# Graph network kernel: the bin builder's products, with the values put on the place one-hots in place of the column one-hots

## The chip, the cores and the metric

One core of a Trainium2 chip runs the whole kernel. The metric is the device time of one execution in microseconds (us). A core has a matrix engine (PE), a vector engine (DVE), a scalar engine (ACT), a general engine (POOL, GpSimd) and an engine that only issues transfers (SP), which run side by side and meet at semaphores.

## What is computed

Three layers of a relational graph convolution over 6,250 nodes with 128 features, 100,000 edges and 4 relations, then the input is added and a layer norm taken. For every layer:

```
for r in range(N_REL):
    mask = (edge_type == r).astype(x.dtype)
    s = segment_sum(x_src * mask[:, None], dst, num_segments=N_NODES)
    c = segment_sum(mask, dst, num_segments=N_NODES)
    mean = s / maximum(c, 1.0)[:, None]
    out = out + mean @ W[r]
```

The edges come sorted by destination. The destinations are drawn so that low node numbers have many edges each and high ones few.

## The kernel before, in words

The 100,000 edges are cut into 782 tiles of 128, and four tiles make a group. Nodes are cut into 49 blocks of 128. Each layer sums its messages in two ways.

**The gathered way** serves the edges of high destinations. POOL gathers, tile by tile, the rows of the table `ytab` (the messages x W[r] of each node and relation, in DRAM) that the edges name: line 796, one instruction a tile, 1450 in all, 550 in layer 0, 458 in layer 1 and 442 in layer 2. They land in a ring of 9 groups; POOL may overwrite a place only when PE has used it (semaphore `s_pe`). DVE builds a weighted one-hot of each tile (line 1452), PE multiplies it by the gathered rows (line 961), and DVE adds the result to the node sums (line 1474). A layer's gathers can only start when the table of that layer has been stored (lines 571 and 575).

**The dense way** serves the first 85 groups, those of low destinations. They are cut into 11 windows of destinations (5 used in layer 0, 10 in layer 1, 11 in layer 2). For a window the kernel builds the counts of edges from each source to each destination and relation (lines 1504, 1505, 1059), keeps them as f16 in DRAM (`a_dram`) for the later layers, and multiplies them with the node features (line 1043).

To build the counts of a window, its edges must first be sorted into bins by source block. This is the **bin builder**, which the change touches. A window has c slots of 128 edges for each of the 49 source blocks, so n = 49c columns: n = 147 in the first window (26 groups), 98 in the second (11 groups), 49 in the others (48 groups). Every edge has a column (`colc`, which slot), a place in the slot (`place[:, 0]`, 0 to 127), two values to be stored there (`vals`: the source within its block, and relation and destination), and its relation (`tmask`). For each group of four tiles:

- DVE (`bins`, lines 1486 to 1491) writes, in f16 with the four tiles innermost, the one-hot of the column (`pbe`, 4n elements a partition), the one-hot of the place (`pbp`, 512), the one-hot of the node within the window (`pbn`, 512), and then the column one-hot times each of the two values (`pbc`, twice 4n). The last two wait for `pbe` alone (`s_v3`). Two buffers alternate, so the first operation waits until PE has used the group before the last (`s_pu`).
- PE (`pe_bins`, lines 1013 and 1014) adds up, for each tile, the place one-hots (as weights, 128x128) times the 2n weighted columns into the bank `psB`, and beside them the relation mask (4 columns of weights) times `pbn`, which counts edges.

When a window's groups are through, DVE takes the bins out of `psB` (`take`, "N" in the order).

The order of all this is fixed when the program is built: `schedule` writes one list per layer of the steps S (a gathered group), P (a bin group), C (a piece of dense products), E, R, A and others, by costs and due times of its own, and all engines follow it. The bin groups 0 to 58 are built by DVE in layer 0, 59 to 81 in layer 1 and 82 to 84 in layer 2, one ahead of PE. The change does not touch `schedule`.

Of the kernel before, what the change touches and what calls it, by code (L numbers as in the profile page):

```python
# [11 lines left out]
F16 = mybir.dt.float16  # L12
F32R = mybir.dt.float32r
ALU = mybir.AluOpType
# [3 lines left out]
P = 128  # L18
D = 128
NR = 4  # L20
# [271 lines left out]
def rgcn_kernel(nc, x, src, dst, typ, weights, roots, biases, c_ident, c_iota, c_tri, c_col, c_need,  # L292
# [3 lines left out]
    NP, NG, NT, NB, NSL, TH = pl.NP, pl.NG, pl.NT, pl.NB, pl.NSL, pl.TH  # L296
# [12 lines left out]
    NPB = 2  # L309
# [13 lines left out]
    width = [c * NB for _, _, c in pl.win]  # L323
# [78 lines left out]
    with ctx:  # L402
        sb = lambda name, shape, dt=F32: ctx.enter_context(nc.sbuf_tensor(name, shape, dt))
# [19 lines left out]
        irep = sb("irep", [P, 4 * max([P] + width)], F16)  # L423
# [16 lines left out]
        vals = sb("vals", [P, 2, TH], F16)  # L440
        colc = sb("colc", [P, TH], F16)
        place = sb("place", [P, 2, TH], F16)
# [19 lines left out]

        WB = W * NB
        OH = NO * ((1 + NR) * P + 4) // 2
        PBW = 8 * P + 8 * max(width)
        V = sb("V", [P, max(NR * P + OH + 2 * max(width) + NPB * PBW // 2, 4 * WB + 4 * TH + P // 2 + 4 * (NP + 2) + TH // 2)])
        cap, tot, offs, adj = (V[:, i * WB:(i + 1) * WB] for i in range(4))
        blk, tmpi, tmp2 = (V[:, 4 * WB + i * TH:4 * WB + (i + 1) * TH].bitcast(I32) for i in range(3))
        relw = V[:, 4 * WB + 3 * TH:4 * WB + 4 * TH]
        ident16 = V[:, 4 * WB + 4 * TH:4 * WB + 4 * TH + P // 2].bitcast(F16)  # L470
        rowt = V[0:2, 4 * WB + 4 * TH + P // 2:4 * WB + 4 * TH + P // 2 + 4 * (NP + 2)].rearrange("r (a b c) -> r a b c", a=2, b=2)
        blk16 = V[:, 4 * WB + 4 * TH + P // 2 + 4 * (NP + 2):4 * WB + 4 * TH + P // 2 + 4 * (NP + 2) + TH // 2].bitcast(F16)
        ms = V[:, 0:NR * P]
        oh = V[:, NR * P:NR * P + OH].bitcast(F16).rearrange("p (v c) -> p v c", v=NO)
        ohs, ohk = oh[:, :, 0:P + 1], oh[:, :, P + 2:(1 + NR) * P + 3]


        by4 = lambda z: z.rearrange("p (c i) -> p c i", i=4)
        PB0 = NR * P + OH + 2 * max(width)
        pbe = lambda n: by4(V[:, NR * P + OH:NR * P + OH + 2 * n].bitcast(F16))  # L480
        pb = V[:, PB0:PB0 + NPB * PBW // 2].bitcast(F16).rearrange("p (v c) -> p v c", v=NPB)
        pbp = lambda v: by4(pb[:, v, 0:4 * P])
        pbn = lambda v: by4(pb[:, v, 4 * P:8 * P])
        pbc = lambda v, n: by4(pb[:, v, 8 * P:8 * P + 8 * n])
        st = sb("st", [P, 4, 6])
        mv = sb("mv", [P, 4, 2])
        sd = sb("sd", [P, 4])
# [40 lines left out]
        psD, psB = ps("psD", [P, 512]), ps("psB", [P, 512])  # L528
# [8 lines left out]
        q = {n: sem(n) for n in names}  # L537
# [408 lines left out]
        def pe_fast(e):  # L946
# [4 lines left out]
            for li, items in enumerate(layers):  # L951
                for pos, it in enumerate(items):
                    if it[0] == "S":
# [9 lines left out]
                        last.then_inc(q["s_pe"], 1)  # L963
                    elif it[0] == "P":
                        pe_bins(e, it[1], it[2])
                    elif it[0] == "E":
                        pe_block(e, li + 1, it[1])
# [30 lines left out]
        def pe_bins(e, w, g):  # L998


            a, b, _ = pl.win[w]
            n, v = width[w], g % NPB
            if g == a and w:
                e.wait_ge(q["s_n1"], w)
                li = [li for li in range(NL) if w in pl.built[li]][0]
                taken = [v for v in range(pl.W[li]) if pl.second[li][v]]
                if taken:
                    e.wait_ge(q["s_fd"], f_no[li, ("F", taken[-1])] + 1)
            e.wait_ge(q["s_pb"], g + 1)
            for i in range(4):  # L1010
                t = 4 * g + i
                first, end = t == 4 * a, t == 4 * b - 1
                e.matmul(psB[:, 0:2 * n], pbp(v)[:, :, i], pbc(v, n)[:, :, i], start=first, stop=end, skip_group_check=True)  # L1013
                last = e.matmul(psB[0:NR, 3 * P:4 * P], tmask[:, t, :], pbn(v)[:, :, i],
                                start=False, stop=end, skip_group_check=True)
            last.then_inc(q["s_pu"], 1)
# [422 lines left out]
        def dve_fast(e):  # L1439
# [36 lines left out]
            def bins(g):  # L1476

                w = [w for w, (a, b, _) in enumerate(pl.win) if a <= g < b][0]
                n, v = width[w], g % NPB
                if g >= NPB:  # L1480
                    e.wait_ge(q["s_pu"], g - NPB + 1)
                if g:
                    e.wait_ge(q["s_pb"], g)
                of4 = lambda z, c: z[:, 4 * g:4 * g + 4].unsqueeze(1).to_broadcast([P, c, 4])
                done[0] += 1
                e.tensor_tensor(pbe(n), by4(irep[:, 0:4 * n]), of4(colc, n), ALU.is_equal).then_inc(q["s_v3"], 1)
                e.tensor_tensor(pbp(v), by4(irep[:, 0:4 * P]), of4(place[:, 0, :], P), ALU.is_equal)
                e.tensor_tensor(pbn(v), by4(irep[:, 0:4 * P]), of4(place[:, 1, :], P), ALU.is_equal)
                e.wait_ge(q["s_v3"], done[0])
                for a in range(2):  # L1490
                    last = e.tensor_tensor(pbc(v, n)[:, a * n:(a + 1) * n, :], pbe(n), of4(vals[:, a, :], n), ALU.mult)  # L1491
                last.then_inc(q["s_pb"], 1)

            built = [0]
# [70 lines left out]
            for n in range(SHEAD):  # L1565
                build(n)
            y_stored(e, 0)
            bins(0)
            lb, pending = 0, None
            for li, items in enumerate(layers):  # L1570
                for pos, it in enumerate(items):
# [3 lines left out]
                    if it[0] == "S":  # L1575
                        n = sbase[li] + it[1]
# [5 lines left out]
                    elif it[0] == "P":  # L1582
                        if it[2] + 1 < pl.G1[-1]:
                            bins(it[2] + 1)
                        ahead(li, pos)
                    elif it[0] == "N":
                        take(it[1])
                    elif it[0] == "C" and it[1] in pl.built[li]:
                        onehots(first_of[it, "end"])
                    elif it[0] == "R":  # L1590
                        k = it[1]
                        e.wait_ge(q["s_acc"], added(li, pos))
                        b = B[:, P * k:P * k + bw[k]]
                        e.tensor_scalar(b, b, 0.0, None, ALU.max).then_inc(q["s_xt"], 1)
                    elif it[0] == "X":
                        parts = x_parts(e, it)
                        e.wait_ge(q["s_xa"], x_no[it] + 1)
                        for o, s_in in parts:
                            last = e.tensor_tensor(o(1), s_in, o(0), ALU.subtract)
                        last.then_inc(q["s_xw"], 1)  # L1600
                    elif it[0] == "F":
                        w = it[1]
                        f = f_no[li, it]
                        ahead(li, pos)
                        e.wait_ge(q["s_dn"], piece_no[li, ("C", w, NPC - 1)] + 1)
                        e.wait_ge(q["s_mb"], f + 1)
                        e.tensor_tensor(ms, banks_of(li, w)[:], ms, ALU.mult).then_inc(q["s_fd"], 1)
                    elif it[0] == "L":
                        last_stage(lb, it)
                        pending = (lb, it)  # L1610
                        lb += 1
# [192 lines left out]
```

## Time and profile before

| | |
|---|---|
| median of 3 runs | 2088.03 us (2086.58 to 2091.99) |
| profiled execution, its own time | 2091.99 us |
| its span | 2090.2 us |
| granted clock of PE, mean | 0.879 |
| busy | PE 1652.7, DVE 1359.6, POOL 1480.7, ACT 1141.2 us |
| instructions | 29086 |

The span is what the profile covers; the time of an execution holds a little more. "Busy" is the time in which an engine had an instruction of the program under way. DVE's instructions overlap at their ends, so the time that a run of them takes is read from the start of its first to the start of the next operation.

### The profile page before, as it was taken

Reading aid. Unit: us, or ns where it says so; the run is one execution under the profiler, and the core shown is the slowest. Engines: PE = TensorE matmul, PEld = TensorE weight load, DVE = VectorE, ACT = ScalarE, POOL = GpSimd, SP = SyncE. Lnnn points to the kernel's source line nnn. Section 1 sums busy time; section 2 is a strip of 40 time slices with the busy share of each in tenths; the row PEclk is TensorE's granted clock in tenths of the full one; section 3 lists DMA queues with packets and bytes.
Section 4 is the critical chain, followed back from the end, with each engine's and each line's share of the span. In section 5 each row is a group of like instructions: output and inputs, shape, how many; then the busy total and the mean of one; then the engine's idle time right before and its main releaser. Section 6 shows DMA issues by size and latency. Waiting matters only on the chain.

```text
span 2090.2 us, 29086 instructions
## 1 busy us (share of the span) xinstructions
PE 1652.7 (79%) x8296; PEld 1169.6 (56%) x8296; DVE 1359.6 (65%) x4230; ACT 1141.2 (55%) x1679; POOL 1480.7 (71%) x1459
## 2 busy tenths in 40 slices
PE   6702657788899999769999988987769999997743
PEld 3402544344456666547876655655458777775543
DVE  4797866799999988424259988876234252446752
ACT  4511000144566788367858768776367677664500
POOL 1088778877777777647777777777377777777774
PEclk9955666799999999889999999999879999999855
DMA  6411222133344455487855445444488777763431
GB/s 204 159 34 34 72 61 64 58 127 104 124 140 147 157 175 188 135 276 248 269 161 172 169 146 177 159 160 162 139 274 261 236 247 249 238 217 105 142 89 51
DMA packets 169224, 330.76 MB, mean 158 GB/s; under 512 B 34704, under 2 KB 85648, under 8 KB 169060
## 3 DMA queue, kind: packets, MB, share of 16 engines
q1 hardware_dynamic: 119000, 230.27, 31.8%
q0 software_dynamic: 46400, 94.97, 16.2%
q10 hardware_dynamic: 3660, 3.60, 0.7%
q8 instruction: 71, 1.16, 0.2%
q14 instruction: 93, 0.76, 0.1%
HBM read 210.05 MB, written 118.65 MB: 157 GB/s over the span
## 4 chain that ended last, share of the span: by engine, by line
POOL 40%; DVE 21%; PE 18%; issue 14%; DMA 3%; DVEq 1%; ACTq 1%; ACT 1%; SPq 0%; POOLq 0%
POOL ring L796 40%; DVE V L1505 5%; DVE S L1452 4%; PE psB L1043 4%; PE psD L1043 3%; DVE V L1504 3%; DMA ring<-ytab,idxc 2%; PE psY L838 2%; PE psGR L961 2%; PE psRB L961 1%; DVE rows L1300 1%; DVE node L1474 1%; DVEq L1460 1%; DMA hrows<-yst 1%; PE psT L838 1%
## 5 line engine op out<-in xcount | busy, mean ns | idle before, releaser
L796 POOL DMA_INDIRECT ring<-ytab,idxc x1402 | 1410.5, 1006 | 576.1 <-issue 419.7
L1043 PE MATMUL psD<-afull,xs 128*128 128x512 f32 (+1 forms) x1862 | 618.6, 459 | 30.3 <-ACT afull L1128 11.8
L1452 DVE TENSOR_SCALAR S<-odd_f,relc,wc 128x129 f32<-128x129 f32 x1450 | 480.6, 398 | 29.3 <-PE psGR L961 20.3
L1128 ACT ACTIVATE afull<-aring 128x1024 fp32r<-128x1024 f16 (+1 forms) x375 | 367.3, 1032 | 126.5 <-PE psD L1043 54.9
L1043 PEld LDWEIGHTS psD<-afull,xs 128*128 128x128 f32 (+1 forms) x1862 | 359.5, 198 | 96.3 <-ACT afull L1178 20.0
L1505 DVE TENSOR_SCALAR V<-odd_h,recs 128x513 f16<-128x513 f16 x686 | 325.0, 474 | 0.0
L961 PE MATMUL psRB<-S,ring 128*128 128x128 f32 (+1 forms) x1440 | 224.6, 305 | 102.6 <-DMA ring<-ytab,idxc 90.5
L1178 ACT ACTIVATE afull<-psT 128x512 fp32r<-128x512 f32 x355 | 205.2, 593 | 179.6 <-PE psT L1059 177.7
L1182 ACT ACTIVATE aring<-afull 128x1024 f16<-128x1024 f32 x275 | 286.1, 1040 | 25.5 <-ACT afull L1178 0.7
L961 PE MATMUL psGR<-S,ring 128*128 128x128 f32 x1364 | 212.4, 306 | 102.3 <-DMA ring<-ytab,idxc 93.0
L961 PEld LDWEIGHTS psRB<-S,ring 128*128 128x128 f32 (+1 forms) x1440 | 205.3, 214 | 131.6 <-issue 86.4
L961 PEld LDWEIGHTS psGR<-S,ring 128*128 128x128 f32 x1364 | 195.9, 215 | 128.2 <-issue 102.5
L1504 DVE TENSOR_SCALAR V<-odd_h,recs 128x129 f16<-128x129 f16 x686 | 189.0, 276 | 25.6 <-PE psT L1059 16.1
L1043 PE MATMUL psB<-afull,xs 128*128 128x512 f32 x686 | 177.2, 407 | 21.1 <-ACT afull L1128 12.7
L1059 PE MATMUL psT<-V 128*128 128x512 f16 x451 | 170.7, 400 | 22.3 <-DVE V L1505 17.2
L1043 PEld LDWEIGHTS psB<-afull,xs 128*128 128x128 f32 x686 | 128.3, 194 | 47.8 <-issue 12.9
L1178 ACT ACTIVATE afull<-psY 128x512 fp32r<-128x512 f32 x184 | 109.1, 593 | 64.4 <-PE psY L1059 63.6
L1474 DVE TENSOR_TENSOR node<-node,psRB 128x128 f32 x192 | 55.0, 287 | 100.4 <-DVE node L1474 58.4
L1474 DVE TENSOR_TENSOR node<-node,psGR 128x128 f32 x198 | 56.8, 287 | 89.8 <-DVE node L1474 58.0
L1158 ACT ACTIVATE xs<-yst 128x512 fp32r<-128x512 f32 (+1 forms) x39 | 23.2, 596 | 167.0 <-DMA yst<-in_x 151.2
L1013 PE MATMUL psB<-V 128*128 128x98 f16 (+2 forms) x340 | 110.8, 326 | 2.2 <-DVE V L1491 2.2
L1059 PEld LDWEIGHTS psT<-V 128*128 128x128 f16 x451 | 42.9, 99 | 108.1 <-issue 58.5
(207 smaller groups left out, 1580.8 us busy)
## 6 DMA issues: line engine op xcount, KB each, us to landing
aring<-a_dram SPq DMA_DIRECT2D x180, 512.0 KB
a_dram<-aring SPq DMA_DIRECT2D x132, 512.0 KB
ytab<-yst SPq DMA_DIRECT2D x144, 256.0 KB
ring<-ytab,idxc POOLq DMA_INDIRECT x1402
hrows<-yst SPq DMA_DIRECT2D x96, 64.0 KB
yst<-hrows SPq DMA_DIRECT2D x24, 256.0 KB, 4.6
yst<-in_x SPq DMA_DIRECT2D x23, 256.0 KB, 4.2
out<-yst SPq DMA_DIRECT2D x11, 256.0 KB, 2.7
```

The source lines that it names most:

```text
L796: e.indirect_dma_start(rows_at(n, i, m), None, Y[li % 2], bass.IndirectOffsetOnAxis(ap=idxc[0:m, t:t + 1], axis=0)).then_inc(landed(n), 16)
L961: last = e.matmul(o, rows_at(n, i, m), S[0:m, n % NS, i, 0:P], start=(i == 0), stop=(i == len(tiles[g]) - 1))
L1013: e.matmul(psB[:, 0:2 * n], pbp(v)[:, :, i], pbc(v, n)[:, :, i], start=first, stop=end, skip_group_check=True)
L1043: last = e.matmul(bank[:], xs[0:m, s, i, :], a, start=(i == 0 and s == 0), stop=(i == NB - 1 and s == 1))
L1059: e.matmul(tbank(u)[:], ohs[:, v % NO, 0:P], ohk[:, v % NO, 0:NR * P], start=(j == 0), stop=(j == c - 1)).then_inc(q["s_bd"], 1)
L1128: e.activation(afull[:, n % AF, 0:m, :], aring[:, cc % AS, o:o + m, :], ACT.Copy).then_inc(q["s_cv"], 1)
L1178: e.activation(afull[:, n % AF, j, :], tbank(u)[:], ACT.Copy).then_inc(q["s_tA"], 1)
L1182: e.activation(aring[:, cc % AS, half:half + m, :], afull[:, n % AF, 0:m, :], ACT.Copy).then_inc(q["s_cv"], 1)
L1452: last = e.tensor_scalar(run3(S[:, n % NS, i, 0:P + 1]), odd128f, relc[:, t:t + 1], wc[:, t:t + 1], ALU.is_equal, ALU.mult)
L1474: e.tensor_tensor(w, w, part[bank][:, j * P:(j + 1) * P], ALU.add).then_inc(q["s_acc"], 1)
L1504: e.tensor_scalar(run3(ohs[:, v % NO, :]), odd128, recs[:, 0, at:at + 1], None, ALU.is_equal)
L1505: e.tensor_scalar(run3(ohk[:, v % NO, :]), odd512, recs[:, 1, at:at + 1], None, ALU.is_equal).then_inc(q["s_oh"], 1)
```

## The change

The two values are multiplied onto the one-hot of the place, not onto the one-hot of the column. The column one-hot (`pbc`, now 4n elements) is the streamed operand of both values, and each value has place one-hots of its own as weights (`pbp(v, 0)` and `pbp(v, 1)`). In the bin builder DVE now makes five operations of 512, 512, 4n, 512 and 512 elements, where it made 4n, 512, 512, 4n and 4n. PE now makes, for each tile, two products of n columns with different weights where it made one of 2n. The numbers that reach `psB` are the same. The buffer V is cut anew for it: `pbe` has 512 elements in place of 4n, a set of `pb` has 12P + 4n in place of 8P + 8n.

```diff
-        PBW = 8 * P + 8 * max(width)
+        PBW = 12 * P + 4 * max(width)
...
-        pbe = lambda n: by4(V[:, NR * P + OH:NR * P + OH + 2 * n].bitcast(F16))
+        pbe = by4(V[:, NR * P + OH:NR * P + OH + 2 * P].bitcast(F16))
...
-        pbp = lambda v: by4(pb[:, v, 0:4 * P])
-        pbn = lambda v: by4(pb[:, v, 4 * P:8 * P])
-        pbc = lambda v, n: by4(pb[:, v, 8 * P:8 * P + 8 * n])
+        pbp = lambda v, a: by4(pb[:, v, 4 * P * a:4 * P * (a + 1)])
+        pbn = lambda v: by4(pb[:, v, 8 * P:12 * P])
+        pbc = lambda v, n: by4(pb[:, v, 12 * P:12 * P + 4 * n])
...
-                e.matmul(psB[:, 0:2 * n], pbp(v)[:, :, i], pbc(v, n)[:, :, i], start=first, stop=end, skip_group_check=True)
+                for a in range(2):
+                    e.matmul(psB[:, a * n:(a + 1) * n], pbp(v, a)[:, :, i], pbc(v, n)[:, :, i],
+                             start=first and a == 0, stop=end, skip_group_check=True)
...
-                e.tensor_tensor(pbe(n), by4(irep[:, 0:4 * n]), of4(colc, n), ALU.is_equal).then_inc(q["s_v3"], 1)
-                e.tensor_tensor(pbp(v), by4(irep[:, 0:4 * P]), of4(place[:, 0, :], P), ALU.is_equal)
+                e.tensor_tensor(pbe, by4(irep[:, 0:4 * P]), of4(place[:, 0, :], P), ALU.is_equal).then_inc(q["s_v3"], 1)
                 e.tensor_tensor(pbn(v), by4(irep[:, 0:4 * P]), of4(place[:, 1, :], P), ALU.is_equal)
+                e.tensor_tensor(pbc(v, n), by4(irep[:, 0:4 * n]), of4(colc, n), ALU.is_equal)
                 e.wait_ge(q["s_v3"], done[0])
                 for a in range(2):
-                    last = e.tensor_tensor(pbc(v, n)[:, a * n:(a + 1) * n, :], pbe(n), of4(vals[:, a, :], n), ALU.mult)
+                    last = e.tensor_tensor(pbp(v, a), pbe, of4(vals[:, a, :], P), ALU.mult)
                 last.then_inc(q["s_pb"], 1)
```

## Rows read from the trace of the kernel before

**Rows 1.** The page, busy time by engine and the chain that ended last.

```profile
PE 1652.7 (79%) x8296; PEld 1169.6 (56%) x8296; DVE 1359.6 (65%) x4230; ACT 1141.2 (55%) x1679; POOL 1480.7 (71%) x1459
...
POOL 40%; DVE 21%; PE 18%; issue 14%; DMA 3%; DVEq 1%; ACTq 1%; ACT 1%; SPq 0%; POOLq 0%
```

**Rows 2.** Waits of POOL: engine line, waited for, us in total, times, longest.

```profile
POOL ring L796 <- issue: 419.7, 1377, 0.3
...
POOL ring L796 <- DMA hrows<-yst: 51.9, 2, 28.7
...
POOL ring L796 <- PE psGR L961: 5.5, 12, 2.0
...
POOL ring L796 <- PE psRB L961: 4.2, 10, 1.4
```

**Rows 3.** Timeline of POOL, no bins near: start, us, operation, idle before.

```profile
1401.56 0.94 POOL L796 DMA_INDIRECT ring<-ytab,idxc  x1 [0.30 <-issue]
```

**Rows 4.** The chain by line, for 389:640, 640:806 and 806:884 us.

```profile
by line: DVE V L1505 33.4%; DVE S L1452 18.8%; DVE V L1504 17.0%; issue 4.0%; DVE node L1474 3.8%; DVEq L1460 3.8%; DVE V L1491 3.2%; DVE V L1487 2.4%; DVE V L1488 2.4%; DMA ring<-ytab,idxc 1.8%; DVE V L1486 1.6%; PE psGR L961 1.2%; DVE cin
...
by line: DVE V L1505 18.1%; DVE S L1452 17.0%; PE psD L1043 11.0%; DVE V L1504 9.1%; DVE node L1474 4.5%; issue 4.4%; DVEq L1460 4.2%; PE psGR L961 4.0%; PE psT L1059 3.8%; PE psRB L961 3.4%; PE psB L1014 2.5%; PE psY L1059 2.3%; PE psT L83
...
by line: POOL ring L796 74.3%; issue 24.0%; DMA ring<-ytab,idxc 3.2%; PE psGR L961 0.7%
```

**Rows 5.** Line 796 by window: window, length, busy (count), PE clock, DMA, GB/s.

```profile
220.00:389.00 169.00, 135.17 (x112) 0.68 0.21 60
...
389.00:511.00 122.00, 94.88 (x90) 0.90 0.33 108
...
511.00:770.00 259.00, 196.79 (x195) 0.97 0.43 144
...
1048.00:1350.00 302.00, 230.74 (x234) 0.98 0.49 163
...
1350.00:1489.00 139.00, 105.17 (x112) 0.90 0.46 152
```

**Rows 6.** Timeline in layer 1, a bin group with n = 49.

```profile
1168.06 0.26 DVE L1486 TENSOR_TENSOR V<-irep,colc 128x196 f16<-128x196 f16 x1
...
1168.20 1.95 POOL L796 DMA_INDIRECT ring<-ytab,idxc  x1 [0.30 <-issue]
...
1169.24 0.28 DVE L1504 TENSOR_SCALAR V<-odd_h,recs 128x129 f16<-128x129 f16 x1
```

**Rows 7.** Timeline in layer 0, bin groups with n = 147.

```profile
342.29 0.47 DVE L1486 TENSOR_TENSOR V<-irep,colc 128x588 f16<-128x588 f16 x1 [4.23 <-PE psB L1014]
...
342.93 0.97 POOL L796 DMA_INDIRECT ring<-ytab,idxc  x1 [0.30 <-issue]
...
344.09 1.35 DVE L1452 TENSOR_SCALAR S<-odd_f,relc,wc 128x129 f32<-128x129 f32 x4
...
345.46 3.19 POOL L796 DMA_INDIRECT ring<-ytab,idxc  x1 [0.30 <-issue]
```

**Rows 8.** Timeline of DVE in layer 0, a bin group with n = 98.

```profile
442.34 0.35 DVE L1486 TENSOR_TENSOR V<-irep,colc 128x392 f16<-128x392 f16 x1
...
443.83 0.40 DVE L1452 TENSOR_SCALAR S<-odd_f,relc,wc 128x129 f32<-128x129 f32 x1
```

**Rows 9.** Groups by form on DVE: count, busy us, mean ns, idle before.

```profile
L1488 DVE TENSOR_TENSOR V<-irep,place 128x512 f16<-128x512 f16 x85 | 35.6, 419 | 0.0
...
L1491 DVE TENSOR_TENSOR V<-V,vals 128x196 f16<-128x196 f16 x96 | 20.4, 253 | 0.0
...
L1486 DVE TENSOR_TENSOR V<-irep,colc 128x588 f16<-128x588 f16 x26 | 12.0, 460 | 32.1 <-PE psB L1014 32.0
```

**Rows 10.** PE: the weight load by form, and the timeline at n = 49.

```profile
L1013 PEld LDWEIGHTS psB<-V 128*128 128x128 f16 x340 | 39.6, 117 | 44.1 <-issue 8.7 <-DVE V L1491 2.8
...
698.19 0.26 PE L1013 MATMUL psB<-V 128*128 128x98 f16 x1
...
698.38 0.28 PE L1014 MATMUL psB<-V,tmask 128*4 128x128 f16 x1
```

More of the change, by code:

```diff
@@ L464, in rgcn_kernel @@
         OH = NO * ((1 + NR) * P + 4) // 2
-        PBW = 8 * P + 8 * max(width)
-        V = sb("V", [P, max(NR * P + OH + 2 * max(width) + NPB * PBW // 2, 4 * WB + 4 * TH + P // 2 + 4 * (NP + 2) + TH // 2)])
+        PBW = 12 * P + 4 * max(width)
+        V = sb("V", [P, max(NR * P + OH + 2 * P + NPB * PBW // 2, 4 * WB + 4 * TH + P // 2 + 4 * (NP + 2) + TH // 2)])
         cap, tot, offs, adj = (V[:, i * WB:(i + 1) * WB] for i in range(4))
@@ L478, in rgcn_kernel @@
         by4 = lambda z: z.rearrange("p (c i) -> p c i", i=4)
-        PB0 = NR * P + OH + 2 * max(width)
-        pbe = lambda n: by4(V[:, NR * P + OH:NR * P + OH + 2 * n].bitcast(F16))
-        pb = V[:, PB0:PB0 + NPB * PBW // 2].bitcast(F16).rearrange("p (v c) -> p v c", v=NPB)
-        pbp = lambda v: by4(pb[:, v, 0:4 * P])
-        pbn = lambda v: by4(pb[:, v, 4 * P:8 * P])
-        pbc = lambda v, n: by4(pb[:, v, 8 * P:8 * P + 8 * n])
+        pbe = by4(V[:, NR * P + OH:NR * P + OH + 2 * P].bitcast(F16))
+        pb = V[:, NR * P + OH + 2 * P:NR * P + OH + 2 * P + NPB * PBW // 2].bitcast(F16).rearrange("p (v c) -> p v c", v=NPB)
+        pbp = lambda v, a: by4(pb[:, v, 4 * P * a:4 * P * (a + 1)])
+        pbn = lambda v: by4(pb[:, v, 8 * P:12 * P])
+        pbc = lambda v, n: by4(pb[:, v, 12 * P:12 * P + 4 * n])
         st = sb("st", [P, 4, 6])
```

## The prediction, made before the change was run

> **What bounds the kernel now.** I read the page first: no engine is busy for more than 79% of the span, and the chain that ended last is 40% GpSimd (POOL), 21% DVE, 18% PE [rows 1]. Shares do not say which of them holds the end, so I asked what POOL waits for. Over the whole run its gathers wait 52 us at the two changes of layer and only 5.5 + 4.2 us for PE to give a ring place back; all the rest before a gather is its own 0.30 us of issue, 1377 times [rows 2]. Undisturbed, a gather takes 0.94 us and 0.30 of issue ahead of it, so one starts every 1.25 us [rows 3]. So inside a layer POOL hardly ever stands still, and whatever lengthens a gather moves the end of the layer. The chain taken by stretches agrees in part: at the end of layer 0 it is POOL and issue; from 389 to 640 us it is DVE (one-hots L1504 and L1505, weighted one-hots L1452), and from 640 to 806 us DVE and PE by turns [rows 4]. I read this as DVE and PE falling behind the gathers until the ring of 9 groups is full, where the few waits of [rows 2] come from, and then catching up.
>
> **What lengthens a gather.** The windows of line 796 give its time by stage [rows 5]. Without bin building (1350 to 1489 us) 112 gathers are busy 105.2 us, 0.94 each. With it they take more; the surplus over 0.944 each, divided by the groups built there:
> - 220 to 389 us, 26 groups with n = 147: 135.2 - 105.7 = 29.4 us, 1.13 a group.
> - 389 to 511 us, 11 groups with n = 98: 94.9 - 85.0 = 9.9 us, 0.90 a group.
> - 511 to 770 us, 22 groups with n = 49: 196.8 - 184.1 = 12.7 us, 0.58 a group.
> - 1048 to 1350 us, 23 groups with n = 49: 230.7 - 220.9 = 9.8 us, 0.43 a group.
>
> The timelines show how: a gather that starts 0.14 us into the five two-input f16 operations of a bin group takes 1.95 us, not 0.94 [rows 6], and one that starts under such a run in the widest window takes 3.19, while another, started 0.64 us into its run, takes 0.97 [rows 7]. So these operations stop a gather, depending on where its start falls in the run. Groups that start in the same place of the gather's beat lose more the longer the run is: runs last (start of the first to start of the next other operation) 1.18 us at n = 49 [rows 6], 1.49 at n = 98 [rows 8], 1.80 at n = 147 [rows 7], and lose 0.50 (the mean over 45 groups, 22.5 / 45), 0.90 and 1.13. That is a slope of 1.3 us of gather per us of run, then 0.74, 1.03 over all.
>
> The Trainium skill (SBUF — State Buffer, the practical consequences) says that a DVE instruction with two SBUF inputs contends with a GpSimd instruction that reads SBUF, and that the loser is blocked until the DVE operation ends. The trace agrees as far as [rows 6] go. The same section adds that tensor_tensor was seen not to stall DMA, by inference because writing descriptors needs the other interface; by that sentence the gathers here would lose nothing before or after and the sum would be 2093 us in place of 2105, and the trace does not bear it out [rows 6].
>
> **The change on DVE.** Per group of four tiles the operations stay five. Elements before: 4n (L1486), 512 (L1487), 512 (L1488), 2 x 4n (L1491), so 1024 + 12n. After: 512, 512, 4n, 2 x 512, so 2048 + 4n. The difference is 1024 - 8n: +632 at n = 49, +240 at n = 98, -152 at n = 147. By form the 512-element operation takes 419 ns and the 196-element one 252 or 253 [rows 9]: 166 / 316 = 0.53 ns an element. The runs show the same, 0.31 us for 588 elements between n = 49 and 98, and again to 147 [rows 6 to 8]. So a run grows by 0.335 us (n = 49, 48 groups: 22 in layer 0, 23 in layer 1, 3 in layer 2), by 0.127 (n = 98, 11 groups) and shrinks by 0.081 (n = 147, 26 groups). DVE busy: 16.1 + 1.4 - 2.1 = +15.4 us.
>
> **The change on POOL.** This is the term that counts. At a slope of 1 the gathers lose what the runs gain: layer 0 gets 22 x 0.335 + 1.4 - 2.1 = 6.7 us, layer 1 7.7, layer 2 1.0, together 15.4. The bounds come from the two measured slopes. A run of n = 49 becomes 1.51 us, a hair over the n = 98 run of today that loses 0.90, so read off there the loss grows by 0.41 a group: 48 x 0.41 + 11 x 0.17 - 26 x 0.06 = 20 us. With the flat slope of 0.74: 48 x 0.25 + 1.0 - 2.2 = 11 us. I take slope 1, between them, because the number of groups behind 0.90 is only 11. Below nothing the term can go only if the places of the starts are redrawn; see the rivals.
>
> Where DVE sets the pace (389 to 640 us), its run growth, 11 x 0.127 and some ten groups x 0.335, 4.7 us, is of the same size as what POOL loses there, and the two run side by side: it is counted once.
>
> **The change on PE.** Each tile's product of 2n columns (L1013) becomes two of n with different weights. The columns that stream are the same; 340 weight loads of 128x128 are added, 117 ns each by the load's row [rows 10]: 39.8 us of PE, or 0.47 a group. If the load is hidden behind the matmul before, it costs nothing. The whole step of today's L1013 at n = 49, its load and its 98 columns, takes 0.19 us from its start to that of the next matmul (698.19 to 698.38) [rows 10], so a load that is added cannot cost more: 0.76 a group is the far end. PE is covered wherever the chain is POOL, by the ring: POOL waits for PE 9.7 us in the whole run. Without that cover it would be the 39.8 us. The one place where it is short is before 640 us in layer 0: there 11 + 10 groups x 0.47 = 9.9 us are added on PE, 5.2 more than on DVE. The chain of that stretch is DVE's and not PE's [rows 4], so I let 1.5 us through, with 0 and 5.2 as ends (at the far price of 0.76: 21 x 0.76 - 4.7 = 11.3). After it 12 x 0.47 = 5.6 us are added on PE against 4.0 on POOL, up to 1.6 more at the tail of the layer, which I leave to the range.
>
> **Costed at nothing.** The order of the operations in a group (the flag that the multiplies wait for is still that of the first), the smaller buffer V (456 bytes a partition less), the smaller PSUM regions: the same bank, the same number of waits, nothing new queued behind one. DVE's L1486 waits 32.0 us for PE to free a bin buffer in the 26 widest groups [rows 9]; PE's added loads lengthen that wait, and the gathers, which set that stage's pace, hide it (uncovered it would be 26 x 0.47 = 12 us).
>
> **Sum.** Against the profiled execution's own 2091.99 us: + 15.4 + 1.5 = 2108.9, +17 us. That execution is 4.0 us above the median of the three runs, so on the median's basis 2088.0 + 17 = 2105 us, 0.8% slower. What this kernel's measurement can tell from no change is about 0.3%, 6.3 us.
>
> **Rivals.**
> - **The steep slope**: every n = 49 group loses what n = 98 loses today. For it: the measured step from 1.18 to 1.49 us. Against: 11 groups. 20 + 1.5: 2110 us, and with the PE end 2114.
> - **PE sets the pace in layer 0**: the added loads are not hidden and both 5.2 and 1.6 us land. For it: PE is 79% busy over the span, more than DVE's 65% [rows 1]. Against: before 640 us the chain names DVE [rows 4]. 2088 + 15.4 + 6.8 = 2110 us, and 2088 + 15.4 + 11.3 = 2115 at the far price of a load.
> - **No contention from these operations**: the long gathers come from something else that falls together with the bin groups. Then POOL loses nothing more, and only the stretch that DVE paces grows, by 4.7 us: 2093 us, within 0.3%. For it: some runs leave a gather at 0.97 us [rows 7]. Against: the surplus grows with n and is nil where no bins are built [rows 5]. The Trainium skill's sentence on tensor_tensor and DMA, above, would be this case.
> - **The flat slope or less**: 11 us on POOL, nothing on PE, 2099 us; with a lucky redraw of starts (a group's loss scatters from 0.03 to 2.25 us [rows 7], about 0.7 for 85 groups, so some 6 us over all) it reaches 2093.
> - **Faster: a redraw of where the 26 widest groups meet the gathers.** They lose 29.4 us, and a run met late, like the 0.97 us gather of [rows 7], costs 0.03. The change shortens these runs and shifts everything around them. If nearly all fell that way, 2088 + 17 - 29 = 2076 us. It decides from 23 us gained, four fifths of the loss; nothing in the change aims the starts, and four times the 6 us scatter is needed.
>
> **How the numbers follow.** Forecast (2098 to 2112) 0.50, steep slope 0.15, PE 0.15, flat or less 0.12 (half of it within 0.3%), no contention 0.04, faster 0.04. Slower 0.50 + 0.15 + 0.15 + 0.06 = 0.86; same 0.10; faster 0.04. The range goes from 2093 (flat slope less the scatter, no PE, or no contention) to 2088 + 20 + 5.2 + 6, 2119 us, with a microsecond at the lower end: 2092 to 2119. The forecast's own is 2098 to 2112.
>
> **What the profile after would show.** Right: runs of the five operations of 1.51 us at n = 49; DVE busy up by 15; gathers' busy time up by 11 to 20, of it about 1 us lost a group in windows like [rows 5] against 0.50; the widest window a little better; undisturbed gathers still 1.25 us apart; POOL's wait for PE under 15 us. 340 more loads on PE and its busy time up. Wrong: gathers' busy time unchanged (no contention), POOL waiting tens of us for PE or a tail longer than 23 to 29 us at the layers' ends (PE is the bound), or the 220 to 389 us stage shorter by 20.

## The result, and the profile after

The changed kernel takes 2107.64 us at the median of four runs (2102.64 to 2108.51) and 2105.48 us at the median of all its twelve (2101.37 to 2108.51), beside 2089.23 us for the kernel before on the same occasions. The ratio, taken over the twelve, is 1.0078, 95% interval 1.0062 to 1.0093, which is 16.3 us (13.0 to 19.4) slower. The profiled execution took 2101.77 us, the second lowest of the twelve, and against the profiled execution of before (2091.99 us) it shows 9.8 us and not 16. So this one profile holds less of the change's cost than most executions do; how executions of one kernel differ is part of the story below.

The page of the changed kernel, busy time by engine and the chain by engine; they answer to [rows 1]:

```profile
PE 1663.6 (79%) x8636; PEld 1191.4 (57%) x8636; DVE 1375.2 (65%) x4230; ACT 1141.7 (54%) x1679; POOL 1486.7 (71%) x1459
...
POOL 47%; PE 17%; issue 15%; DVE 14%; DMA 3%; DVEq 1%; ACT 1%; ACTq 1%; SPq 0%; POOLq 0%
```

DVE has 15.6 us more (the sum said 15.4), PE 340 more matmuls and loads but only 10.9 us more, POOL 6.0 us more, less than the 11 to 20 that the prediction gave as a sign of being right. POOL's waits, against [rows 2]:

```profile
POOL ring L794 <- DMA hrows<-yst: 53.6, 2, 28.5
...
POOL ring L794 <- PE psGR L959: 6.1, 12, 2.7
POOL ring L794 <- PE psRB L959: 2.7, 7, 0.8
```

8.8 us of waiting for PE after, 9.7 before: PE is no more in the way than it was. (Lines shift: the gather is line 794 now, the gathered products 959, the bin products 1012. DVE's L1486 makes the one-hot of the place now, L1487 that of the node, L1488 that of the column.) The gathers by stage, the stages cut where the bin groups of the changed kernel start and end, against [rows 5]:

```profile
221.00:384.00 163.00, 128.87 (x113) 0.66 0.22 63
384.00:504.00 120.00, 92.89 (x90) 0.90 0.34 109
504.00:767.00 263.00, 201.87 (x192) 0.96 0.42 141
1050.00:1357.00 307.00, 236.31 (x233) 0.97 0.48 159
1357.00:1497.00 140.00, 105.86 (x113) 0.91 0.46 154
```

The last row is a stage without bins, 0.94 us a gather as before. In the others take 0.944 us for each gather off the busy time and divide by the groups, as before:

| stage | surplus before | after | a group, before | after |
|---|---|---|---|---|
| n = 147, 26 groups | 29.4 us | 22.2 | 1.13 | 0.85 |
| n = 98, 11 groups | 9.9 | 7.9 | 0.90 | 0.72 |
| n = 49, layer 0, 22 groups | 12.7 | 20.6 | 0.58 | 0.94 |
| n = 49, layer 1, 23 groups | 9.8 | 16.4 | 0.43 | 0.71 |

An n = 49 group costs the gathers 0.82 us (37.0 / 45) where it cost 0.50: +0.32, where the forecast said 0.335. The widest groups cost 7 us less in all, where it said 2. The ends of a window cut gathers in two, which moves a surplus by up to about 2 us; and the four surpluses together grow by only 5.3 us here, since the 7.2 and 2.0 us less of the wide groups stand against 7.9 and 6.6 more.

A bin group with n = 49 in layer 1, timelines of DVE and of POOL, against [rows 6]:

```profile
1113.14 0.42 DVE L1486 TENSOR_TENSOR V<-irep,place 128x512 f16<-128x512 f16 x1
1113.48 0.42 DVE L1487 TENSOR_TENSOR V<-irep,place 128x512 f16<-128x512 f16 x1
1113.81 0.26 DVE L1488 TENSOR_TENSOR V<-irep,colc 128x196 f16<-128x196 f16 x1
1113.98 0.76 DVE L1491 TENSOR_TENSOR V<-V,vals 128x512 f16<-128x512 f16 x2
1114.65 0.28 DVE L1504 TENSOR_SCALAR V<-odd_h,recs 128x129 f16<-128x129 f16 x1
```

```profile
1113.32 2.24 POOL L794 DMA_INDIRECT ring<-ytab,idxc  x1 [0.30 <-issue]
1115.87 0.94 POOL L794 DMA_INDIRECT ring<-ytab,idxc  x1 [0.30 <-issue]
```

The run lasts 1.51 us (1113.14 to 1114.65), 1.18 before. The gather that starts 0.18 us into it ends at 1115.56, 0.91 us after the run is over. The gather of [rows 6] ended at 1170.15, and its run at 1169.24: 0.91 us again. A gather that is caught like this does not share the time with the run: its last 0.91 us come after the run. So its length follows the run's end: 0.33 us more of run and a start 0.04 us later make 0.29 us more of gather.

On PE, the tile of the changed kernel at n = 49, against [rows 10]:

```profile
1112.38 0.15 PEld L1012 LDWEIGHTS psB<-V 128*128 128x128 f16 x2
1112.38 0.27 PE L1012 MATMUL psB<-V 128*128 128x49 f16 x2
...
1112.58 0.08 PEld L1014 LDWEIGHTS psB<-V,tmask 128*4 128x4 f16 x1
```

Both products together take 0.20 us from their start to that of the next matmul, where the one product took 0.19. Over all tiles of the two traces the medians are 0.194 us against 0.191 at n = 49, 0.279 against 0.277 at n = 98 and 0.367 against 0.365 at n = 147. The second load costs the stream next to nothing.

### The profile page after: what moved, and what is told of

It reads as the page before. It is cut to its first block, busy times and chain, and to the rows that moved or that the text cites. A ratio compares the mean times of both kernels' runs of the same rounds, so it can differ in the third digit from the quotient of the medians.

```text
span 2099.9 us, 29766 instructions
## 1 busy us (share of the span) xinstructions
PE 1663.6 (79%) x8636; PEld 1191.4 (57%) x8636; DVE 1375.2 (65%) x4230; ACT 1141.7 (54%) x1679; POOL 1486.7 (71%) x1459
## 4 chain that ended last, share of the span: by engine, by line
POOL 47%; PE 17%; issue 15%; DVE 14%; DMA 3%; DVEq 1%; ACT 1%; ACTq 1%; SPq 0%; POOLq 0%
POOL ring L794 44%; DVE V L1505 5%; PE psD L1043 4%; PE psB L1043 3%; DVE S L1452 3%; POOL rows L794 3%; PE psY L836 3%; DVE V L1504 3%; DMA ring<-ytab,idxc 2%; PE psGR L959 2%; PE psRB L959 1%; DVEq L1460 1%; PE psT L836 1%; DVE node L1474 1%; DMA hrows<-yst 1%
## 5 line engine op out<-in xcount | busy, mean ns | idle before, releaser
L1043 PE MATMUL psB<-afull,xs 128*128 128x512 f32 x686 | 178.5, 409 | 20.8 <-ACT afull L1128 12.1
L1012 PE MATMUL psB<-V 128*128 128x49 f16 (+2 forms) x680 | 111.7, 250 | 2.2 <-DVE V L1491 2.2
```

The costliest lines, as they stand in the source:

```text
L1012: e.matmul(psB[:, a * n:(a + 1) * n], pbp(v, a)[:, :, i], pbc(v, n)[:, :, i], start=first and a == 0, stop=end, skip_group_check=True)
L1043: last = e.matmul(bank[:], xs[0:m, s, i, :], a, start=(i == 0 and s == 0), stop=(i == NB - 1 and s == 1))
```

## The experiments

The ratio is that to the kernel before on the same chip, with its 95% interval; us are the ratio's difference times 2089. "POOL busy" is from the page of each profile (before: 1480.7 us), one execution each.

| run | ratio | us against before | POOL busy |
|---|---|---|---|
| the change | 1.0078 (1.0062 to 1.0093) | +16.3 | 1486.7 |
| e1 PE part only | 1.0010 (0.9998 to 1.0023) | +2.1 | 1482.4 |
| e2 DVE part only | 1.0063 (1.0046 to 1.0079) | +13.2 | 1495.5 |
| e3 one-input operations | 0.9722 (0.9705 to 0.9739) | -58.1 | 1415.7 |
| e4 put apart | 0.9819 (0.9802 to 0.9836) | -37.8 | 1434.9 |
| e5 one more operation | 1.0095 (1.0080 to 1.0110) | +19.8 | 1503.0 |
| e6 the change, put apart | 0.9854 (0.9839 to 0.9868) | -30.5 | 1434.1 |
| e7 short breaks | 0.9825 (0.9811 to 0.9839) | -36.6 | 1431.0 |
| e8 widest groups only | 0.9979 (0.9970 to 0.9989) | -4.4 | 1473.1 |
| e9 the change, short breaks | 0.9883 (0.9865 to 0.9901) | -24.4 | 1436.2 |
| e10 apart and breaks | 0.9815 (0.9796 to 0.9834) | -38.7 | 1430.1 |

The expectations speak of "52 us" lost to bin groups. That is a slip: 52.0 us are the three of layer 0, and the four surpluses of [rows 5] add up to 61.8 us.

**e1, the PE part alone.** The kernel before, each product split in two with the same weights loaded twice.

```diff
-                e.matmul(psB[:, 0:2 * n], pbp(v)[:, :, i], pbc(v, n)[:, :, i], start=first, stop=end, skip_group_check=True)
+                for h in range(2):
+                    e.matmul(psB[:, h * n:(h + 1) * n], pbp(v)[:, :, i], pbc(v, n)[:, h * n:(h + 1) * n, i],
+                             start=first and h == 0, stop=end, skip_group_check=True)
```

> The kernel before, with each tile's product of 2n columns made as two of n columns that load the same place one-hots anew: the 340 extra loads and matmuls of the change, nothing of its DVE work; the output is unchanged. Contention theory (the change costs because DVE's runs of two-input operations hold the gathers up): within 0 to 5 us of before, the gathers' busy time unchanged, PE busy up by up to 40 us. Rival (PE sets the pace in layer 0): 7 us or more slower.

+2.1 us, and the interval reaches from 0.4 us faster to 4.8 slower: it excludes the rival's 7. Extra busy time on PE is 4.5 us on its page of the profile, not 40.

**e2, the DVE part alone.** The changed kernel, with the two products made one again.

```diff
-                for a in range(2):
-                    e.matmul(psB[:, a * n:(a + 1) * n], pbp(v, a)[:, :, i], pbc(v, n)[:, :, i],
-                             start=first and a == 0, stop=end, skip_group_check=True)
+                e.matmul(psB[:, 0:2 * n], pbp(v, 0)[:, :, i], pbc(v, n)[:, :, i].unsqueeze(1).to_broadcast([P, 2, n]),
+                         start=first, stop=end, skip_group_check=True)
```

> The changed kernel, with one product of 2n columns a tile as before: the place one-hots of the first value are the weights and the column one-hots are streamed twice by a repeated read; the second value is left out, so the bins hold the first value twice. Contention theory: all of the change's cost but 0 to 5 us, 13 to 18 us slower than before, an n = 49 group's gathers lose about 0.8 us as in the changed kernel. Rival (PE): less than half of the change's cost, under 9 us.

+13.2 us (9.6 to 16.5), at the lower end of the expected 13 to 18, and POOL's busy time up by 14.8. With e1 that makes 15.3 of the 16.3 us. The cost lies in DVE's operations, and reaches the end through POOL. The gathers by stage, stages cut at this kernel's own bin groups:

```profile
220.00:387.00 167.00, 132.93 (x112) 0.67 0.21 61
387.00:508.00 121.00, 94.49 (x88) 0.90 0.33 107
508.00:775.00 267.00, 206.81 (x197) 0.97 0.42 142
1053.00:1360.00 307.00, 235.89 (x234) 0.97 0.48 159
```

The surpluses over 0.944 us a gather are 27.2, 11.4, 20.8 and 15.0 us, where they were 29.4, 9.9, 12.7 and 9.8: -2.2 for the widest groups, +1.5 at n = 98, +8.1 and +5.2 at n = 49 (0.80 us a group, as expected), 12.6 us in all. DVE does the same work here as in the changed kernel, and the wide groups do not give back the 7.2 and 2.0 us that they gave back in the profile of that.

**e3, one-input operations in place of the two-input ones.** Edit of the kernel before; the buffers are also set to zero once.

```diff
-                e.tensor_tensor(pbe(n), by4(irep[:, 0:4 * n]), of4(colc, n), ALU.is_equal).then_inc(q["s_v3"], 1)
...
+                big, small = {1: 2, 2: 2, 3: 4}[n // NB], {1: 2, 2: 4, 3: 1}[n // NB]
+                for k in range(big):
+                    last = e.tensor_scalar(run3(pb[:, v, 514 * k:514 * k + 513]), odd512, 1.0, None, ALU.is_equal)
+                for k in range(small):
+                    o = 514 * big + 130 * k
+                    last = e.tensor_scalar(run3(pb[:, v, o:o + 129]), odd128, 1.0, None, ALU.is_equal)
```

> The kernel before, with the five two-input f16 operations of a group replaced by one-input tensor_scalar operations on f16 of about the same total length (1.16 us at n = 49, 1.54 at 98, 1.75 at 147; the forms of lines 1504 and 1505), which write the same buffers with other values: the bins are left out. Contention theory: no gather is held up any more; of the 52 us lost to bin groups the 29 of the widest windows and the 9.8 of layer 1 come back whole, of layer 0 after 389 us only a part since DVE sets the pace there: 35 to 50 us faster than before. Rival (the long gathers come from something else that falls together with the bin groups): within 5 us of before.

The gathers by stage, stages cut at this kernel's own bin groups:

```profile
215.00:365.00 150.00, 113.73 (x120) 0.70 0.26 74
365.00:473.00 108.00, 81.61 (x87) 0.95 0.37 119
473.00:736.00 263.00, 192.71 (x204) 0.99 0.44 149
1002.00:1299.00 297.00, 224.46 (x239) 0.98 0.50 167
```

0.94 or 0.95 us a gather in each of them: the stalls are gone. But DVE's runs are not as long as the expectation says, which adds up single operations that overlap at their ends. One at n = 49, timeline of DVE:

```profile
1046.56 0.74 DVE L1487 TENSOR_SCALAR V<-odd_h 128x513 f16<-128x513 f16 x2
1047.22 0.34 DVE L1490 TENSOR_SCALAR V<-odd_h 128x129 f16<-128x129 f16 x2
1047.48 0.28 DVE L1503 TENSOR_SCALAR V<-odd_h,recs 128x129 f16<-128x129 f16 x1
```

From start to start it lasts 0.92 us, where it was 1.18 before; the others last 1.17 and 1.44, where they were 1.49 and 1.80, and DVE is busy 25.8 us less. So this run changes the kind of the operations and their length together. By the prediction's slope of 1 the length alone would give back some 25 us of gathers (an estimate from these lengths), and POOL is busy 65.0 us less; the kernel is 58 us faster, more than the 35 to 50 expected. The third rival of the prediction, no contention, falls. How much of the 58 us DVE's own lighter work gave is not separated here; e4 and e7 leave all of DVE's operations in.

**e4, the same operations put one by one between others.** The core of the edit (`first`, `weigh` hold the operations of a group and their waits; `one` pops one of them, and is called after each tensor_scalar of line 1452 and after each pair of lines 1504 and 1505; whatever is left is made before the next group).

```diff
+            def one():
+                if todo:
+                    todo.pop(0)()
...
+                todo.append(first)
+                todo.append(lambda: e.tensor_tensor(pbp(v), by4(irep[:, 0:4 * P]), of4(place[:, 0, :], P), ALU.is_equal))
+                todo.append(lambda: e.tensor_tensor(pbn(v), by4(irep[:, 0:4 * P]), of4(place[:, 1, :], P), ALU.is_equal))
+                todo.append(lambda: weigh(0))
+                todo.append(lambda: weigh(1))
```

> The kernel before, with the same five operations of a group, but put one by one between DVE's other operations (after each tensor_scalar of lines 1452, 1504 and 1505), so that runs are broken up wherever such an operation follows; the output is unchanged. Contention theory in its present form (a gather that meets a run waits for the end of the run): stalls shrink from the length of a run to that of one operation, 15 to 35 us faster than before. Rival (a gather is delayed by the sum of the two-input operations, in whatever order): within 5 us of before. Second rival (more gathers meet an operation, and each waits for a fixed time beside it): slower.

A group in layer 1, timeline of DVE:

```profile
1042.04 0.42 DVE L1511 TENSOR_TENSOR V<-irep,place 128x512 f16<-128x512 f16 x1
1042.37 0.40 DVE L1452 TENSOR_SCALAR S<-odd_f,relc,wc 128x129 f32<-128x129 f32 x1
1042.69 0.41 DVE L1512 TENSOR_TENSOR V<-irep,place 128x512 f16<-128x512 f16 x1
1043.02 0.40 DVE L1452 TENSOR_SCALAR S<-odd_f,relc,wc 128x129 f32<-128x129 f32 x1
```

37.8 us faster, a little more than the 15 to 35 expected, and 45.8 us less on POOL with the same DVE operations (1358.5 us busy, 1359.6 before). Most of what these operations cost comes from their standing in unbroken runs, not from how much of them there is.

**e5, one more operation in each run.** A dose: 0.34 us more in all 85 runs.

```diff
+                e.tensor_tensor(by4(spare[:].bitcast(F16)), by4(irep[:, 0:4 * P]), of4(place[:, 0, :], P), ALU.is_equal)
                 e.tensor_tensor(pbp(v), by4(irep[:, 0:4 * P]), of4(place[:, 0, :], P), ALU.is_equal)
```

> The kernel before, with one more two-input f16 operation of 512 elements in each group's run (the place one-hot is made twice, once into a spare buffer); the output is unchanged. Every run grows by 0.34 us, in all 85 groups. Contention theory: the gathers lose 0.74 to 1.0 us per us of run, 21 to 29 us slower than before. Rival (a longer run costs only where DVE sets the pace): 21 groups x 0.34, about 7 us slower.

+19.8 us (16.7 to 23.0), just under the expected 21 to 29: 0.69 us for each of the 28.9 us of run added (85 x 0.34), 0.77 by POOL's busy time (+22.3). The rival's 7 us is out. The slope of 1 does not hold for all widths; the table by layer, below, shows where it does.

**e6, the change with its operations put apart** as in e4 (edit as there, with the change's five operations).

> The changed kernel, with its five operations of a group put one by one between DVE's other operations, as in the fourth run; the output is unchanged. Contention theory (the change costs because its runs are longer, and a gather waits for the end of a run): most of the 18 us goes away with the runs; what stays is DVE's 5 us before 640 us and a little for the longer single operations, 3 to 10 us above the fourth run, 2057 to 2064 us. Rival (the added two-input time costs by its sum, in whatever order): 15 us or more above the fourth run.

-30.5 us against before, 7.3 above e4 by the ratios (6.7 by the medians, 2060.43 and 2053.77 us, of two occasions): inside the 3 to 10 expected, and less than half of what the change costs unbroken. Its POOL busy time, 1434.1 us, is that of e4, 1434.9: put apart, the change's longer operations cost the gathers nothing in these two profiles.

**e7, tiny operations between the five.** Each writes one element a partition and reads one.

```diff
+                def mark(k):
+                    e.tensor_scalar(spare[:, 4 * g + k:4 * g + k + 1], epst[:], 1.0, None, ALU.mult)
                 e.tensor_tensor(pbe(n), by4(irep[:, 0:4 * n]), of4(colc, n), ALU.is_equal).then_inc(q["s_v3"], 1)
+                mark(0)
                 e.tensor_tensor(pbp(v), by4(irep[:, 0:4 * P]), of4(place[:, 0, :], P), ALU.is_equal)
+                mark(1)
...
                 for a in range(2):
+                    mark(2 + a)
```

> The kernel before, with one tiny one-input operation (one element a partition) between each two of a group's five operations; the output is unchanged. If a gather that waits gets in at any gap between two-input operations: most of the 52 us of stalls comes back, less four tiny operations a group on DVE (some 0.07 us each, 24 us in all, of which some 6 to 10 stand where DVE sets the pace): 2060 to 2080 us. If it needs a gap of some length, as DVE's full-size operations give it in the fourth run: no gain, and up to 10 us slower than before.

-36.6 us, as good as e4, and better than the 2060 to 2080 us expected (2053.89). DVE is busy 18.0 us more than before and PE 7.7 less, POOL 49.7 less. A group of the widest window, timelines of DVE and of POOL:

```profile
313.90 0.47 DVE L1489 TENSOR_TENSOR V<-irep,colc 128x588 f16<-128x588 f16 x1 [4.36 <-PE psB L1015]
314.29 0.14 DVE L1488 TENSOR_SCALAR spare<-epst 128x1 f32<-128x1 f32 x1
314.35 0.42 DVE L1491 TENSOR_TENSOR V<-irep,place 128x512 f16<-128x512 f16 x1
```

```profile
313.99 1.20 POOL L797 DMA_INDIRECT ring<-ytab,idxc  x1 [0.30 <-issue]
```

This gather starts 0.09 us into the run and takes 1.20 us. In the kernel before, one that meets an unbroken run of this width near its start, timelines of DVE and of POOL:

```profile
252.73 0.45 DVE L1486 TENSOR_TENSOR V<-irep,colc 128x588 f16<-128x588 f16 x1
```

```profile
252.99 2.43 POOL L796 DMA_INDIRECT ring<-ytab,idxc  x1 [0.30 <-issue]
```

It starts 0.26 us into its run and takes 2.43 us. The gather of e7 ends at 315.19, 0.90 us after the tiny operation starts at 314.29; from there to the start of the next two-input operation, 314.35, are 0.06 us, and they are enough.

**e8, the change in the 26 widest groups alone** (all of its parts, chosen by `n > P`; elsewhere the code of before).

> The kernel before, with the change made only for the 26 groups with n = 147, where it shortens the run from 1.80 to 1.72 us and puts the 588-element operation third; the output is unchanged. By the slope of 1 of the prediction: 2 us faster, not to be told from none. Rival (the order and lengths within the run decide which gathers slip in between, as the changed kernel's profile with 8 us less of stalls in these groups suggests): 5 to 9 us faster.

-4.4 us (-6.3 to -2.3): clear of nothing. The slope's 2 us lie just outside the interval and the rival's 5 to 9 mostly too, so the run does not decide between them. POOL's busy time falls by 7.6 us.

**e9, the change with tiny operations between.** Edit as in e7.

> The changed kernel with one tiny one-input operation between each two of a group's five operations, as in the seventh run; the output is unchanged. If a gather waits for the end of a run only, the change's longer runs cost nothing once they are broken, and what stays of the change is DVE's and PE's work where they set the pace (before 640 us): 3 to 10 us above the seventh run, 2057 to 2064 us. Rival (the added two-input time costs by its sum): 15 us or more above the seventh run.

-24.4 us against before, and 12 above e7 (0.9883 against 0.9825), more than the 3 to 10 expected and less than the rival's 15, so that it bears out neither. POOL's waits in e7 and then in e9:

```profile
POOL ring L797 <- DMA hrows<-yst: 50.6, 2, 27.1
...
POOL ring L797 <- PE psRB L962: 12.9, 19, 3.7
POOL ring L797 <- PE psGR L962: 12.6, 14, 4.2
```

```profile
POOL ring L795 <- DMA hrows<-yst: 59.8, 2, 31.4
...
POOL ring L795 <- PE psRB L960: 15.6, 15, 5.6
...
POOL ring L795 <- PE psGR L960: 12.4, 17, 4.0
```

Waiting at the changes of layer grows by 9.2 us, that for ring places by 2.5, and POOL's busy time by 5.2. I read the waits as work that DVE and PE have left at the end of a layer, which comes to the surface when the gathers are no longer held up; the 5.2 us say that the longer operations still hold gathers a little. Neither is shown: these are one execution each, e9's was its slowest, and which engine it is was not tried.

**e10, put apart, and a tiny operation wherever two would still touch.**

> The kernel of the fourth run (operations put one by one between DVE's others), with a tiny one-input operation wherever two two-input operations would still follow each other; the output is unchanged. The stalls of the widest windows that stayed in the fourth run go, and DVE has few tiny operations to make where it sets the pace: 2 to 10 us faster than the fourth run, 2044 to 2052 us. Rival (DVE's and PE's pace before 640 us already sets the end of layer 0, so that the stalls that are left cost nothing): the same as the fourth run within 2 us.

-38.7 us, 0.9 better than e4 by the ratios: its interval covers most of e4's, so that the expected further gain of 2 to 10 us is not shown and the rival, the same within 2 us, fits. POOL's busy time is 4.8 us lower than in e4, so the shorter stalls did not turn into time that can be measured.

## Why the prediction was right

**The bound.** Right: inside a layer the gathers set the pace. e7 shows it best, with POOL busy 49.7 us less and the kernel 36.6 us faster although DVE is busy 18.0 us more. That the stretch paced by DVE is hidden beside the gathers ("counted once") was not tried by itself; e6 agrees with it, where 7 of the 16 us are left once the stalls are mostly gone.

**The chain view** was a weak witness in one place. Before, it named DVE and PE from 640 to 806 us [rows 4]. After, the same stretch reads:

```profile
by line: POOL ring L794 77.2%; issue 22.2%; PE psRB L959 0.5%; PE psD L1043 0.3%
```

Yet in that stretch POOL waited for PE 2.8 us before and 1.1 us after, and otherwise issued without a stop. I read this as engines that run level there, so that small shifts decide which one the chain goes by. POOL's list of waits [rows 2] was the steadier guide.

**The change on DVE**: forecast +15.4 us busy and runs of 1.51 us; measured +15.6 and 1.51.

**The change on POOL**: forecast 15.4 us, -2.1 for n = 147, +1.4 for n = 98, and +7.4 and +7.7 for n = 49 in layers 0 and 1. By the surpluses e2 has -2.2, +1.5, +8.1 and +5.2, and the changed kernel's own profile -7.2, -2.0, +7.9 and +6.6. The busy time of line 796 (794 in the change and e2, 797 in e5) over whole layers:

| | layer 0 | layer 1 | layer 2 |
|---|---|---|---|
| before | 490.20 | 443.56 | 418.72 |
| the change | 490.30 | 450.94 | 418.97 |
| e2 DVE part only | 498.41 | 450.65 | 420.07 |
| e5 one more operation | 504.43 | 450.50 | 419.28 |

In layer 1, where all groups have n = 49, three kernels whose runs grow by 7.7 or 7.8 us in all give 7.4, 7.1 and 6.9 us: there the slope is close to 1. In layer 0 e5 gives 14.2 us for 59 x 0.34 = 20.1 us of run, a slope of 0.7, and the two kernels with the change's DVE work differ, 0.1 and 8.2 us, where the forecast was 6.7. So the change's profile carries little of the cost in layer 0, and what carries the forecast there is the time of the twelve executions and e2's profile. The term of the widest groups, -2.1, is the least sure one: -7.2 and -2.2 in single profiles of the same DVE work, -4.4 (-6.3 to -2.3) in e8, over eleven executions.

The reason for such scatter shows in gathers that meet a wide run at almost the same place. One of POOL in the kernel before, and then two in the changed one:

```profile
348.95 2.75 POOL L796 DMA_INDIRECT ring<-ytab,idxc  x1 [0.30 <-issue]
```

```profile
334.68 2.67 POOL L794 DMA_INDIRECT ring<-ytab,idxc  x1 [0.30 <-issue]
...
347.31 0.95 POOL L794 DMA_INDIRECT ring<-ytab,idxc  x1 [0.30 <-issue]
```

All three start 0.06 us ahead of a run (DVE's L1486 starts at 349.01, and at 334.74 and 347.37); two are held for 1.7 or 1.8 us, the third not at all, and the last two are in one kernel, with the same operations of DVE before and in the run. Three of 26 groups that flip like this make 5 us. I take this for the reason why executions of one kernel differ and why the profiled execution shows 9.8 us and the twelve together 16.3; with one trace of each kernel that is not shown. What decides a flip, down there in hundredths of a us, is open.

**A row that was misread.** The prediction took the gather of 3.19 us [rows 7] for one that starts under a run of the widest window. It starts at 345.46, and the run at 345.95. What it starts under is another operation with two inputs in SBUF, right ahead of the run, and such an operation holds a gather by itself too. Timelines of DVE, with one that stands alone and then the one of 345.35, and of POOL for the first:

```profile
300.31 0.68 DVE L1599 TENSOR_TENSOR xs<-yst,xs 128x512 fp32r<-128x512 f32 x1
...
345.35 0.69 DVE L1599 TENSOR_TENSOR xs<-yst,xs 128x512 fp32r<-128x512 f32 x1
```

```profile
300.42 1.39 POOL L796 DMA_INDIRECT ring<-ytab,idxc  x1 [0.30 <-issue]
```

So the unbroken stretch of the 3.19 us gather was 2.40 us long (345.35 to 347.75) and not 1.80, and part of the surplus of the widest windows is that of L1599, which the change does not touch.

**The signs in the profile**: runs of 1.51 us, DVE's +15.6 and POOL's 8.8 us of waiting for PE are as forecast. POOL's busy time, forecast 11 to 20 us up, is up 6.0 in the change's profile and 14.8 in e2's.

**The change on PE**: forecast 1.5 us between 0 and 5.2; e1 measured 2.1 (-0.4 to 4.8). The step behind it, 0.47 us a group of added loads on PE, was too large and harmless: the pair of products takes 0.20 us where the one took 0.19.

**The rivals.** No contention: excluded by e3, e4 and e7, and with it the sentence of the Trainium skill (SBUF — State Buffer, Who interferes with whom, practical consequences) that tensor_tensor was seen not to stall DMA, as far as POOL's indirect gathers go. The other sentence there, that a DVE instruction with two SBUF inputs contends with a GpSimd instruction that reads SBUF, agrees with these runs. That the loser is blocked until the DVE operation ends is not borne out for an operation in a run: in [rows 6] the first operation lasts from 1168.06 to 1168.32, and the gather is held until the run's end at 1169.24. PE sets the pace: excluded by e1. The steep slope (0.41 a group at n = 49): 0.32 measured in the change's profile and 0.30 in e2's. The flat one (0.25): e5's slope over all widths, 0.69, is of its size, but n = 49 by itself is closer to 1. The redraw happened in small, on the widest groups of the profiled execution, and did not decide.

**The sum**: 17 us forecast, 16.3 measured (13.0 to 19.4). By experiments it is 13.2 (9.6 to 16.5) for DVE and 2.1 (-0.4 to 4.8) for PE. The mechanism is shown; that the sum agrees within 1 us is closer than these intervals, and partly luck.

## What to carry to other kernels

Where GpSimd issues indirect gathers back to back, look for unbroken runs of DVE operations with two SBUF inputs, and count their length, not only their sum: the same operations put between one-input operations, or with a one-element operation between them, made this kernel about 1.8% faster (e4, e7, e10), which is more than twice what the change lost. A change that moves elements from one operation to another is then priced by what it does to the length of each run, times how often that run occurs (here at 0.7 to 1 us of gather per us of run), and a shape that occurs 48 times outweighs the one in which it saves. One profile can be a lucky draw: the one of the change shows 9.8 us of 16.3, and only e2's agrees with the forecast stage by stage. When the bound is taken away, ask again what was hidden: of the change, 12 us are left with the short breaks (e9 over e7) and 7 with the operations put apart (e6 over e4).

## What the runs showed of the hardware that was not expected

- A caught gather mostly waits for the whole run, not for the operation it met. In the trace before, 68 gathers that meet a run of bins take over 1.0 us. All 45 that take over 1.3 us wait for the run's end, and most of them end 0.90 us after it. 14, none over 1.3 us, end 0.90 us after a boundary between two operations of the run: they got in there. In the changed kernel all 52 of over 1.3 us wait for the end, and 13 shorter ones got in at an inner boundary. With the tiny operations (e7), 57 of 58 such gathers end 0.90 us after the next operation that is not of two SBUF inputs starts.
- What stands right behind a run matters. With L1599 there (two SBUF inputs, 0.60 us from start to start) the end of the gather comes 1.50 us after the run's end and not 0.90 (three gathers before, one after). A one-input operation is not always a break either: L1594, an f32 tensor_scalar of 128x128 that lasts 0.13 us from start to start, behind a run makes it 1.03 or 1.04 us in all four cases of over 1.3 us of the two traces. Timelines of DVE and of POOL in the kernel before:

```profile
727.46 0.22 DVE L1594 TENSOR_SCALAR node<-node 128x128 f32<-128x128 f32 x1
```

```profile
726.67 1.82 POOL L796 DMA_INDIRECT ring<-ytab,idxc  x1 [0.30 <-issue]
```

- A second load of 128x128 f16 weights between two matmuls of 49 columns cost 0.01 us or less of pitch, though such a load is 0.12 us long in the trace.
- Gathers that start 0.06 us ahead of like runs of one kernel can be held for 1.7 us or not at all.
